# Two layers of local attention: q and k turned straight out of PSUM, a head's 128 queries on the partitions, and a new order on every engine

## The reference

```python
x = x + tanh(g_xattn) * cross_attention(layernorm(x), layernorm(ctx))   # 16 x 128 tokens x 128
t = layernorm(x)                                      # enters the stack; the blocks of 128 tokens are independent here
for layer in range(2):
    h = shift_token(t)                                # second half of the channels from the token before
    q, k, v = split(h @ wqkv[layer])                  # 8 heads of 64
    q, k = l2norm(q) * qs, l2norm(k) * ks
    q, k = q*cos*scale + rotate_half(q)*sin*scale, k*cos/scale + rotate_half(k)*sin/scale
    s = 8 * q @ k.T                                   # windows of 64: key j for query i if i-64 <= j <= i
    t = t + (softmax(s) @ v) @ wo[layer]
    h = layernorm(shift_token(t)) @ w1; a, g = split(h)
    t = t + (a * gelu(g)) @ w2
out = x + tanh(g_ffn) * t
```

## Time and profile before

| | |
|---|---|
| median of 3 runs | 484.67 us (484.40 to 484.72) |
| the profiled execution's own time | 486.15 us |
| its span, first to last instruction | 484.3 us, mean granted TensorE clock 0.964 |
| attention of layer 0, of layer 1 | 72.4 to 240.6 us, 275.2 to 448.3 us |
| busy share of the span: PE, DVE, ACT, POOL | 81%, 69%, 67%, 57% |

### The profile page before, as it was taken

The page is one execution under the profiler, slowest core; times in us unless marked ns, Lnnn a source line. Parts: engine busy times, 40 slices in busy tenths (PEclk is TensorE's granted clock), DMA queues, the critical chain, the costliest instruction groups (busy, mean ns, idle before and its releaser), DMA issues.

```text
span 484.3 us, 10003 instructions
## 1 busy us (share of the span) xinstructions
PE 391.6 (81%) x3564; PEld 291.2 (60%) x3564; DVE 332.8 (69%) x1180; ACT 325.4 (67%) x1083; POOL 274.6 (57%) x326
## 2 busy tenths in 40 slices
PE   0676777888898889888799577898989898878795
PEld 0464566677677677766434266776777677755342
DVE  2759778688878887883144656888878887841445
ACT  2356546787888788887422338887888788883424
POOL 5284118778778877884000097788778877841000
PEclk9979898899999999999989969999999999999999
DMA  7900000000000000000000000000000000000003
GB/s 160 312 2 3 1 1 1 1 3 1 1 3 1 1 1 3 1 2 2 0 2 0 0 0 1 1 3 1 1 3 1 2 3 1 1 1 0 2 0 87
DMA packets 10288, 7.42 MB, mean 15 GB/s; under 512 B 3245, under 2 KB 9447, under 8 KB 10238
## 3 DMA queue, kind: packets, MB, share of 16 engines
q1 hardware_dynamic: 8590, 5.63, 4.1%
q0 software_dynamic: 848, 1.15, 1.2%
q10 hardware_dynamic: 800, 0.00, 0.1%
HBM read 5.73 MB, written 1.05 MB: 14 GB/s over the span
## 4 chain that ended last, share of the span: by engine, by line
ACT 41%; DVE 26%; PE 22%; issue 5%; POOL 4%; DMA 1%; SPq 0%; DVEq 0%; ACTq 0%
ACT p L808 9%; PE ps L506 8%; ACT p L824 7%; DVE shared L1030 7%; ACT sqr L683 6%; PE ps L633 4%; DVE h_lo L903 4%; ACT oT L830 3%; ACT kT L841 3%; ACT vv L788 2%; ACT qT L839 2%; ACT rr L692 2%; POOL shared L357 2%; DVE hn L1050 2%; DVE shared L915 2%
## 5 line engine op out<-in xcount | busy, mean ns | idle before, releaser
L374 POOL TENSOR_TENSOR shared<-shared,stab 128x256 f32<-128x256 f32 x128 | 106.9, 865 | 0.0
L357 POOL TENSOR_TENSOR shared<-shared 128x512 f32<-128x512 f32 x64 | 83.5, 1309 | 19.2 <-DVE shared L1030 16.6
L808 ACT ACTIVATE p<-sm,nm 128x128 f32<-128x128 f32 x128 | 50.1, 393 | 40.5 <-DVE nm L1064 40.5
L1030 DVE TENSOR_TENSOR shared<-shared,ctab 128x512 f32<-128x512 f32 x64 | 70.1, 1097 | 0.0
L362 POOL TENSOR_TENSOR p<-p,pri 128x512 f32<-128x512 f32 x32 | 33.3, 1040 | 40.0 <-DVE pri L1083 40.0
L908 DVE TENSOR_REDUCE ss<-sqr 128x16 f32<-128x1024 f32 x32 | 39.0, 1220 | 23.5 <-ACT sqr L683 23.4
L915 DVE TENSOR_TENSOR shared<-ps,rr 128x1024 f32<-128x1024 f32 x32 | 39.2, 1224 | 21.8 <-ACT rr L692 21.8
L262 POOL TENSOR_TENSOR mark_g<-ones 128x1 f32<-128x1 f32 x32 | 6.7, 209 | 79.6 <-DVE shared L915 79.4
L506 PE MATMUL ps<-hn,w1g 128*128 128x512 f32 (+1 forms) x96 | 46.8, 604 | 5.8 <-DVE uu L1107 5.8
L393 PE MATMUL ps<-wqkv_hi,h_hi 128*128 128x512 f32 x96 | 45.2, 471 | 7.6 <-DVE shared L915 6.6
L824 ACT ACTIVATE p<-sm,nm 128x64 f32<-128x64 f32 x128 | 43.0, 351 | 0.0
(11 more groups left out here) (143 smaller groups left out, 976.6 us busy)
## 6 DMA issues: line engine op xcount, KB each, us to landing
wqkv_raw<-in_L_ffn_wqkv_dram SPq DMA_DIRECT2D x1, 1536.0 KB, 15.9
out_dram<-shared SPq DMA_DIRECT2D x4, 256.0 KB, 2.5
w_raw<-in_L_ffn_w_dram SPq DMA_DIRECT2D x1, 682.0 KB
xt<-in_x_dram SPq DMA_DIRECT2D x2, 256.0 KB, 4.6
xt<-in_x_dram SPq DMA_DIRECT2D x1, 512.0 KB, 12.4
wo_raw<-in_L_ffn_wo_dram SPq DMA_DIRECT2D x1, 512.0 KB
ct<-in_ctx_dram POOLq DMA_DIRECT2D x1, 360.0 KB, 10.9
w_raw<-in_L_ffn_w_dram SPq DMA_DIRECT2D x2, 128.0 KB
```

Source lines behind the costliest of these rows:

```text
L357: T(qr[j][:, part], rc1[j][:, part], rs1[j][:, part], ALU.add).then_inc(rot_ready[j], 1)
L374: nc.gpsimd.tensor_tensor(s4[:, s, :, u, :], q4[:, s, :, 1 - u, :], tb, ALU.mult).then_inc(s_ready[j], 1)
L808: A(p1[j][:, c, :], sm1[j][:, c, :], ACT.Exp, bias=nm[j][:, c:c + 1], scale=-1.0, accum_out=psum_[j][:, c:c + 1]).then_inc(p_done[j], 1)
L1030: V.tensor_tensor(rc1[m.j][:, part].rearrange("p (h d) -> p h d", h=HEADS), qn[m.j][:, part].rearrange("p (h d) -> p h d", h=HEADS), ctab[ ...
```

## The change

Queries of a head now lie on the 128 partitions and all 128 keys in the free dimension, masked where the window does not reach, so that a head has one score tile, one maximum and one sum. The turn works on q and k as they come from the projection, in PSUM: VectorE forms the cosine product and both sine products (`turns`), GpSimd adds them (`rotate`). The reciprocal length of q is no longer multiplied in: it is the scale of exp (`weights`), and the shift is the maximum times it (`shifts`). That of k is multiplied into the turned k by GpSimd (`unit_k`). The copies of kT and v out of PSUM move from ScalarE to VectorE (`k_rows`, `v_rows`). The high and low halves of h are formed four batches at a time, the high on VectorE (`high_half`), the low on GpSimd (`low_half`). In the pipeline, the projection of q and k runs four batches ahead (before: three) and the norm ends in the batch's own step (before: two steps later); every engine starts at n = -3 (GpSimd -2), and steps 16 and 17 are empty. The buffers of `gl` and `uu` move. The list of heads is split in two halves a = 0, 1 (even and odd heads).

```diff
-    i = np.arange(128)[:, None] % W
+    i = np.arange(N)[:, None]
     j = np.arange(N)[None, :]
-    m1 = np.where((j >= i) & (j <= i + W), 0.0, NEG)
-    m0 = np.where(j[:, :W] <= i, 0.0, NEG)
-    mask = np.concatenate([m1, m0], 1).astype(np.float32)
+    mask = np.where((j <= i) & (j >= i - W), 0.0, NEG).astype(np.float32)
     return rot, mask, np.eye(128, dtype=np.float32)
...
+            def low_half(gl_):
+                g = gl_ % NG
+                pool.wait_ge(hi_ready, gl_ + 1)
+                T(h_lo[:, g * GB:(g + 1) * GB, :], xs[:, g * GB:(g + 1) * GB, 0:N],
+                  h_hi[:, g * GB:(g + 1) * GB, :].bitcast(F32), ALU.subtract).then_inc(h_ready, 1)
...
+            def normalise(m, a):
+                pool.wait_ge(ri_ready[a], m.i + 1)
+                T(pp[m.j][:, a, :, :], pp[m.j][:, a, :, :],
+                  pri[m.j][:, a * 4:a * 4 + 4].unsqueeze(2).to_broadcast([128, PAIRS, 128]), ALU.mult).then_inc(pn_ready[a], 1)
...
+            def rotate(m, s):
+                part = slice(s * INNER, (s + 1) * INNER)
+                pool.wait_ge((tq_done, tk_done)[s], m.i + 1)
+                T(cs[m.j][:, part], cs[m.j][:, part], sn[m.j][:, part], ALU.add).then_inc((aq_done, ak_done)[s], 1)
...
+            def unit_k(m):
+                k = cs[m.j][:, INNER:2 * INNER].rearrange("p (h d) -> p h d", d=DH)
+                pool.wait_ge(ak_done, m.i + 1)
+                pool.wait_ge(r_ready, m.i + 1)
+                T(k, k, rr[m.j][:, HEADS:2 * HEADS].unsqueeze(2).to_broadcast([128, HEADS, DH]), ALU.mult).then_inc(mk_done, 1)
...
             def step(at, on):
+                if on(0):
+                    normalise(at(0), 0)
                 if on(2):
+                    rotate(at(2), 0)
+                    rotate(at(2), 1)
+                    unit_k(at(2))
                 if on(1):
+                    normalise(at(1), 1)
...
+            def project_q(m):
+                pe.wait_ge(h_ready, m.i // GB + 1)
+                if m.b > 0:
+                    pe.wait_ge(tq_done, m.i)
+                    pe.wait_ge(sqq_done, m.i)
                 qkv(m, 0)
...
+            def scores_(m):
+                pe.wait_ge(qT_ready, m.i + 1)
+                pe.wait_ge(kT_ready, m.i + 1)
+                if m.b > 0:
+                    pe.wait_ge(mx_done[0], m.i)
+                    pe.wait_ge(mx_done[1], m.i)
+                for c in range(PAIRS):
+                    for a in range(2):
+                        r = slice(a * 64, a * 64 + 64)
+                        last = mm(ps[:, SA + a, c * 128:(c + 1) * 128], qT[m.j][r, c, :], kT[m.j][r, c, :], start=True, stop=True)
+                last.then_inc(s_ps, 1)
...
+            def attend(m):
+                if m.b > 0:
+                    pe.wait_ge(hn_ready, m.i)
+                pe.wait_ge(v_ready, m.i + 1)
+                pe.wait_ge(pt_ready[0], m.i + 1)
+                pe.wait_ge(pt_ready[1], m.i + 1)
+                for c in range(PAIRS):
+                    for a in range(2):
+                        h = 2 * c + a
+                        last = mm(ps[a * 64:a * 64 + 64, OB, c * 128:(c + 1) * 128], vv[m.j][:, h * DH:(h + 1) * DH],
+                                  pT[m.j][:, a, c, :], start=True, stop=True)
+                last.then_inc(o_ps, 1)
+            def out_proj(m):
...
             def step(at, on):
+                if on(1):
+                    project_v(at(1))
+                if on(2):
+                    rows_T(at(2), 0)
                 if on(0):
+                    out_proj(at(0))
+                if on(2):
+                    rows_T(at(2), 1)
+                if on(4):
+                    project_q(at(4))
+                if on(0) and not on(3):
                     m = at(0)
+                    c = 2 - m.end + m.i + 1
+                    if c == 0:
+                        pe.wait_ge(layer_w1, m.layer + 1)
+                        pe.wait_ge(tk_done, m.end)
+                        pe.wait_ge(sqq_done, m.end)
+                        hidden(m.layer, 0, 0)
+                    if c == 2:
+                        hidden(m.layer, 0, 1)
+                if on(0):
+                    deviation(at(0))
+                if on(4):
+                    project_k(at(4))
+                if on(0) and not on(1):
+                    hidden(at(0).layer, 0, 2, [0])
+                if on(0):
+                    variance(at(0))
                 if on(1):
+                    weights_T(at(1), 1)
+                    weights_T(at(1), 0)
                 if on(2):
+                    scores_(at(2))
+                if on(1):
+                    attend(at(1))
...
+            def weights(m, a):
+                act.wait_ge(nb_ready[a], m.i + 1)
+                for c in range(PAIRS):
+                    h = 2 * c + a
+                    A(pp[m.j][:, a, c, :], pp[m.j][:, a, c, :], ACT.Exp, bias=nb[m.j][:, a * 4 + c:a * 4 + c + 1],
+                      scale=rr[m.j][:, h:h + 1], accum_out=psum_[m.j][:, a * 4 + c:a * 4 + c + 1]).then_inc(p_done[a], 1)
...
             def step(at, on):
+                if on(3):
+                    squares(at(3), 1)
+                if on(2):
+                    lengths(at(2))
                 if on(3):
                     squares(at(3), 0)
+                if on(0):
+                    heads_out(at(0))
                 if on(1):
+                    weights(at(1), 1)
+                    weights(at(1), 0)
                 if on(0):
+                    dev_square(at(0))
                 if on(2):
+                    q_rows(at(2))
+                if on(0):
+                    dev_rstd(at(0))
+                if on(1):
+                    weights_out(at(1), 1)
+                    weights_out(at(1), 0)
...
-            def squared_norms(m):
-                dve.wait_ge(sq_done[m.j], 2 * m.g + 2)
-                V.tensor_reduce(ss[m.j][:], sqr[m.j][:].rearrange("p (h d) -> p h d", d=DH), AX.X, ALU.add).then_inc(ss_sum[m.j], 1)
-                dve.wait_ge(ss_sum[m.j], m.g + 1)
-                V.tensor_scalar(ssc[m.j][:], ss[m.j][:], 1e-24, None, ALU.max).then_inc(ss_ready[m.j], 1)
...
-            def over_norms(m):
-                dve.wait_ge(r_ready[m.j], m.g + 1)
-                V.tensor_tensor(qn[m.j].rearrange("p (h d) -> p h d", d=DH), ps[:, QB:KB + 1, :].rearrange("p s (h d) -> p (s h) d", d=DH),
-                                rr[m.j][:].unsqueeze(2).to_broadcast([128, 2 * HEADS, DH]), ALU.mult).then_inc(qn_ready[m.j], 1)
...
+            def high_half(gl_):
+                g = gl_ % NG
+                V.tensor_copy(h_hi[:, g * GB:(g + 1) * GB, :], xs[:, g * GB:(g + 1) * GB, 0:N]).then_inc(hi_ready, 1)
...
+            def turns(m, s):
+                dve.wait_ge((q_ps, sqk_done)[s], m.i + 1)
+                x_, done = ps[:, QB + s, :].rearrange("p (h d) -> p h d", d=DH), (tq_done, tk_done)[s]
+                V.tensor_tensor(heads(cs[m.j], s), x_, ctab[:, m.layer, s, :].unsqueeze(1).to_broadcast([128, HEADS, DH]), ALU.mult)
+                for u in range(2):
+                    o_, i_ = slice(u * 32, u * 32 + 32), slice(32 - u * 32, 64 - u * 32)
+                    last = V.tensor_tensor(heads(sn[m.j], s)[:, :, o_], x_[:, :, i_],
+                                           stab[:, m.layer, s, o_].unsqueeze(1).to_broadcast([128, HEADS, 32]), ALU.mult)
+                last.then_inc(done, 1)
...
+            def squared(m, s):
+                dve.wait_ge((sqq_done, sqk_done)[s], m.i + 1)
+                V.tensor_reduce(ss[m.j][:, s * HEADS:(s + 1) * HEADS], heads(sqr[m.j], s), AX.X, ALU.add).then_inc(sq_sum, 1)
+            def clamped(m):
+                dve.wait_ge(sq_sum, 2 * m.i + 2)
+                V.tensor_scalar(ssc[m.j][:], ss[m.j][:], 1e-24, None, ALU.max).then_inc(ss_ready, 1)
...
+            def maxima_(m, a):
+                apart(V, s_ps, m.i + 1, a)
+                for c in range(PAIRS):
+                    last = V.tensor_tensor_reduce(out=pp[m.j][:, a, c, :], in0=ps[:, SA + a, c * 128:(c + 1) * 128], in1=msk[:],
+                                                  scale=1.0, scalar=-3e38, op0=ALU.add, op1=ALU.max,
+                                                  accum_out=mx[m.j][:, a * 4 + c:a * 4 + c + 1])
+                last.then_inc(mx_done[a], 1)
...
+            def shifts(m, a):
+                dve.wait_ge(mx_done[a], m.i + 1)
+                dve.wait_ge(r_ready, m.i + 1)
+                V.scalar_tensor_tensor(out=nb[m.j][:, a * 4:a * 4 + 4], in0=mx[m.j][:, a * 4:a * 4 + 4], scalar=-1.0,
+                                       in1=rr[m.j][:, a:HEADS:2], op0=ALU.mult, op1=ALU.mult).then_inc(nb_ready[a], 1)
+            def inverse(m, a):
+                dve.wait_ge(p_done[a], PAIRS * m.i + PAIRS)
+                V.reciprocal(pri[m.j][:, a * 4:a * 4 + 4], psum_[m.j][:, a * 4:a * 4 + 4]).then_inc(ri_ready[a], 1)
...
+            def k_rows(m):
+                dve.wait_ge(kT_ps, m.i + 1)
```

(32 more changed lines are left out.)

433 lines of the change are left out of this document (125 added, 308 removed).

## The result

The changed kernel takes **493.94 us** (median of 4 runs, 493.03 to 495.64) where the kernel before takes 484.7 beside it: a ratio of 1.017, with a 95% interval of 1.011 to 1.024. The forecast was 479.4 us in a range of 458 to 488, with 0.70 on faster. So it was wrong in its sign, and its range did not hold the time. The profiled execution took 493.86 us, its span is 492.1. The granted clock in what follows is the share of its full speed at which TensorE was allowed to run, 1.00 or 0.50.

A forecast was written before the change was run, and what follows sets the result against it. No engine was taken as full; a loop of waits between batches bounds the kernel. First layer +0.3 and second −5.6 gave −5.3: 480.9 us for the profiled execution, 479.4 on the median's scale, range 458 to 488.

The forecast's parts named there:

- The bound and the loop: Steady attention rounds: the loop of waits from batch to batch decides, repeating every 9.70 us against 9.67 before.
- The lock: VectorE's 16-element maximum L1012 waits for GpSimd's addition each batch, ending at 2.57 instead of 1.58: 1.0 us lost.
- Two steps with the low half: Steps n = 2 and 6 of a layer: the maximum meets normalising, oT sets the exps, 0.45 us less each.
- VectorE's queue: Steady rounds: VectorE's instructions alone, with the blocked maximum, would need 9.43 us a period.
- the walk through the ends: First and last rounds of each attention stretch, timed step by step; first layer's end at 240.95, second's at 442.65.
- two without turns, bound by exps and oT: Two late rounds of the first layer's attention stretch, without turning q and k: 9.0 and 8.3 us, reaching 231.3.
- the first second-half reciprocal comes at 88.8: First layer's start: the first reciprocal L1032 for the second half of the heads, closing the ramp, at 88.8 us.
- at 290.5: Second layer's start: the first such reciprocal at 290.5 us, against 294.70 before, with TensorE's clock low.
- stage D: From the first layer's last hn over the MLP to the second layer's first second-half reciprocal: 49.8 us.
- the lock bites twice: Slower rival, chance 0.12: k's length comes late, the shift L1027 also waits for GpSimd's product; period 10.35, 496 us.
- The maximum slips ahead: Faster rival, chance 0.20: the maximum runs before GpSimd's addition; period 8.9, 20.8 us less, about 460 us.
- B and E: Thirteen steady periods of the first and of the second layer, batch 0 to batch 13: 125.2 us each.

The follow-up runs named there:

- e8_late_maximum: Changed kernel with the 16-element maximum L1012 moved behind v's copy and hn on VectorE, nothing added or removed; 475.85 us, ratio 0.977.
- e4_const_scale: Changed kernel with a constant as the scale of exp instead of q's length read from SBUF (output lacks that length); 475.74 us, ratio 0.978.
- e5_fill_half: Changed kernel plus unread identity matmuls in TensorE's idle time at both ends of each attention stretch and the MLP's start; 478.99 us, ratio 0.986.
- e10_start_only: Changed kernel with the added matmuls of e5_fill_half at the start of each attention stretch alone; 488.72 us, ratio 1.004.

## Why the prediction was wrong

**Right, by its own steps.**
- The bound and the loop: "9.70 us" was 9.66, and thirteen periods took 125.06 and 126.33.
- The lock: "it ends at 2.57 instead of 1.58" was 2.56 (169.46 + 1.03 − 167.93). Its price was shown by e8_late_maximum, which only moves the instruction.
- The copy from PSUM at 0.61 (kT, 168.14 to 168.75), the exps 0.48 apart, the pairs of scores side by side (16 in 1.16).
- Two steps with the low half "0.45 less each": 9.27 against 9.66, so 0.39. The number is right by another path. The maximum did not wait there (0.17 at 112.28), and the exps started at 5.31 of the round behind a shift that GpSimd's product held for 0.64 (115.39), 0.08 after oT.
- VectorE's queue was 0.25 too long, which changed nothing in the forecast but set the price of e4_const_scale.

**Wrong.** The step that failed is the walk through the ends, and in it above all "The last batch still needs normalising, pT, mixing, oT, the projection, residual, 1.9 us of MLP products that stand ahead of its deviation, and the norm: 9.65, end 240.95". Every duration in it was taken from the rows of the steady stretch, at a clock of 1.00. The chain was right to 0.3 us, for it takes 9.99 to the end of hn at that clock (9.70 to its start). At 1.2 GHz it took 13.35 (13.06 to its start). The same holds for "two without turns, bound by exps and oT, take 9.0 and 8.3": they took 8.98 and 8.68 in e5_fill_half, but 10.23 and 8.68 in the changed kernel (the 0.4 in the second is an error of its size at either clock). Likewise for "the first second-half reciprocal comes at 88.8", which was 91.16 (1.1 of the difference in the prologue). For "at 290.5" the text did say that the clock is low, by the kernel before, and the stage D came out only 1.5 above. In sum the measured time lies 13 us above the forecast, nearly all of it outside the steady rounds, and e5_fill_half gives 15 back. It lands at 478.99, beside the 479.4 that was forecast. So near a hit holds some luck: D is 2.6 shorter than forecast, and the first reciprocal comes 3.8 later, 3.6 of it in the prologue.

**The rivals.** None of them named the clock. The time of 496 for "the lock bites twice" is near the result, but its mechanism is not there: the shift took 0.16 in every steady round (above). Only in the two low-half rounds of each layer did one wait, 0.63, and these rounds are the shorter ones. "The maximum slips ahead" gave 460 and a period of 8.9. The period was right (8.91 and 8.96) once the maximum was out of the way, which the change did not do. Its 20.8 us were too many, since only 19 of the 26 rounds have the full gain (13.4 and 12.3 us in B and E of those two runs).

**What should have been seen.** The earlier trace rows give a mean clock of 0.98 for the first attention stretch of the kernel before. With levels of 1.00 and 0.50 that is 4% at the lower one, 7 of 168 us, so the full clock was not to be had for nothing. The change takes a thousand matmuls from TensorE and leaves it waits at the ends, which may be why its mean clock is lower (0.923 against 0.964 in the profiled runs). No run tests that. A second walk of the ends with TensorE's durations doubled would have widened the range by what C shows, 5 us, and by something like it at each of the other ends.

## What to carry to other kernels

Walk the steady period at the clock of the steady rows, but the first and last rounds twice, at both levels of TensorE's clock, and let the range reach to the slower walk. An instruction that GpSimd's work blocks costs what is queued behind it, so before you remove it try to put behind it only what cannot be blocked, and ahead of it what reads PSUM. When a change leaves an engine less to do, look at the granted clock of TensorE before and after, because a busy time that grows while the work shrinks (391.6 to 401.4 us here) can be a sign of a lower one.

## What the runs showed of the hardware

- Added matmuls with no use made this kernel 15 us (3%) faster, and nothing else in its work was changed. The mean granted clock of the profiled runs was 0.923 without them and 0.975 with them.
- The clock can fall in one layer and not in the other, with the same instructions: the last batch took 13.06 and 9.70 us in the changed kernel's profiled run. In that of e10_start_only it took 13.74 and 13.34 (449.88 − 436.54 in the second layer), so both layers had the low clock. The waits ahead of the fall were under 2 us (1.45, 0.88), and the same waits stood where it did not fall.
- The start varies by up to 5 us from one profiled run to the next: the last group's residual in the prologue, whose code is the same in all variants of the changed kernel, lies at 66.7 to 71.8 us. The granted clock in the slices up to there differs among them. That this is the cause was not tried.
- A VectorE instruction of scalar form on 16 elements waits for the end of GpSimd's instruction (1.03 us for 0.17), and so does a small one with two inputs in SBUF (0.53 us for 0.16 on 4 elements). One with a PSUM input does not (0.68 and 0.28 beside it).
